# Eight PSUM banks dealt out anew in a hybrid attention kernel: three side banks and two maximum banks, with narrow pieces of several heads in one bank

## The reference, cut to what matters

```python
x = x + attn_a(_layernorm(x))   # scores = -|pos_q - pos_k| / 4, causal softmax, times V, projection
x = x + ffn(_layernorm(x))      # sigmoid(xr Wr^T) * (relu(xk Wk^T)^2 Wv^T), token shift
x = x + attn_b(_layernorm(x))   # 16 heads of 16: k, q, v = x Wkqv + b
                                # scores = q k^T / 4, causal softmax over keys, times v
x = x + ffn(_layernorm(x))
```

## Time and profile before

| | before |
|---|---|
| median of 3 executions | 2311.16 us (2307.39 to 2319.46) |
| the profiled execution, its own time | 2316.06 us |
| its span, first to last instruction | 2314.3 us |
| TensorE busy, share of the span | 83% |
| VectorE busy | 61% |
| ScalarE busy | 54% |
| GpSimd busy | 44% |

### The profile page before, as it was taken

One profiled execution on the slowest core, in us unless ns is written; L12 is line 12 of the kernel. 1 busy time (PEld: TensorE's weight loads), 2 busy tenths in 40 slices (PEclk: granted clock), 3 DMA queues, 4 the chain that ended last, 5 costly groups with the idle time before them and its releaser, 6 DMA issues. The chain is left out here.

```text
span 2314.3 us, 32515 instructions
## 1 busy us (share of the span) xinstructions
PE 1929.1 (83%) x9842; PEld 936.3 (40%) x9842; DVE 1417.5 (61%) x4173; ACT 1254.3 (54%) x2673; POOL 1024.2 (44%) x1074
## 2 busy tenths in 40 slices
PE   4477888888988899788987889888887889988986
PEld 3344343334433354324543345333443335432423
DVE  2336677567676666666765666756656666677642
ACT  0623654675537555394545755366554855555563
POOL 4454354335642455334743266423654246422414
PEclk8677899989998899989999899998999899999998
DMA  3006011310132111211122011231113111141100
GB/s 96 0 20 117 1 28 42 69 28 15 43 85 34 28 29 53 67 29 28 33 67 64 13 29 37 76 63 28 28 37 83 28 28 28 43 87 29 29 19 19
DMA packets 64347, 97.27 MB, mean 42 GB/s; under 512 B 15655, under 2 KB 58029, under 8 KB 58030
## 3 DMA queue, kind: packets, MB, share of 16 engines
q1 hardware_dynamic: 64174, 95.20, 18.6%
HBM read 61.09 MB, written 33.55 MB: 41 GB/s over the span
## 5 line engine op out<-in xcount | busy, mean ns | idle before, releaser
L852 ACT ACTIVATE pt<-exp_bank 128x512 f32<-128x512 f32 (+3 forms) x1536 | 742.5, 494 | 806.5 <-PE exp_bank L822 797.0
L867 DVE CUSTOM_DVE_ANT_0 max_bank<-max_bank,mask 128x128 f32<-128x128 f32 (+3 forms) x1024 | 500.3, 502 | 495.2 <-PE max_bank L811 478.2
L822 PE MATMUL exp_bank<-qs,ks 98*128 98x512 bf16 (+3 forms) x1536 | 523.8, 347 | 72.5 <-ACT pt L852 66.3
L811 PE MATMUL max_bank<-ks,qs 96*128 96x512 bf16 (+3 forms) x1536 | 525.0, 349 | 24.3 <-DVE piece_max L870 17.2
L870 DVE TENSOR_REDUCE piece_max<-max_bank 128x1 f32<-128x512 f32 x512 | 342.9, 686 | 164.7 <-PE max_bank L811 161.5
L837 PE MATMUL o_bank<-pt,v 128*17 128x512 f32 (+3 forms) x3072 | 346.2, 525 | 8.0 <-ACT pt L852 3.0
L889 POOL TENSOR_SCALAR_AFFINE_SELECT pt<-pt 128x512 f32<-128x512 f32 x256 | 170.1, 664 | 404.2 <-ACT pt L852 403.8
L353 POOL TENSOR_SCALAR xh<-xs,mv,rstd 128x256 f32<-128x256 f32 x256 | 322.6, 1266 | 10.0 <-PE side L379 3.8
L822 PEld LDWEIGHTS exp_bank<-qs,ks 98*128 98x128 bf16 x1536 | 153.9, 101 | 353.4 <-ACT pt L852 229.5
L811 PEld LDWEIGHTS max_bank<-ks,qs 96*128 96x128 bf16 x1536 | 154.7, 101 | 257.9 <-issue 102.1
L544 PE MATMUL side<-vp,p 128*128 128x260 f32 x576 | 185.2, 450 | 33.7 <-ACT p L473 18.3
(11 more groups left out here) (94 smaller groups left out, 2243.0 us busy)
## 6 DMA issues: line engine op xcount, KB each, us to landing
parts_dram<-parts SPq DMA_DIRECT2D x64, 384.0 KB, 2.6
qs<-parts_dram SPq DMA_DIRECT2D x192, 128.0 KB, 7.0
ks<-parts_dram SPq DMA_DIRECT2D x32, 384.0 KB, 4.8
xs<-in_L_attn_a_x_dram SPq DMA_DIRECT2D x16, 512.0 KB, 4.3
ks<-parts_dram SPq DMA_DIRECT2D x32, 256.0 KB, 5.5
out_dram<-xs SPq DMA_DIRECT2D x16, 512.0 KB, 3.1
ks<-parts_dram SPq DMA_DIRECT2D x32, 128.0 KB, 5.9
qs<-neg_maxT SPq DMA_DIRECT2D x64, 8.0 KB, 1.9
```

Of the source, the lines that this page charges most:

```text
L811: pe.matmul(max_bank[u % MAX_BANKS][:, 0:k1 - k0], qs[r][0:KROWS, j, P * tile:P * (tile + 1)], ks[r][0:KROWS, j, k0:k1], start=True, stop= ...
L822: pe.matmul(exp_bank[k % EXP_BANKS][:, 0:q1 - q0], ks[r][:, j, P * kt:P * (kt + 1)], qs[r][:, j, q0:q1], start=True, stop=True).then_inc(s ...
L852: act.activation(pt[:, e % 2, j, 0:q1 - q0], exp_bank[k % EXP_BANKS][:, 0:q1 - q0], ACT.Exp, scale=SCALE).then_inc(exp_done, 1)
L867: dve.tensor_tensor_reduce(scores, scores, mask[:, HALF - w:HALF], 1.0, LOWEST, ALU.add, ALU.max, piece_max[:, j, m:m + 1]).then_inc(max_f ...
```

## The change

The eight PSUM banks were 2 side, 3 maximum, 2 exponential and 1 output bank; they are 3 side, 2 maximum, 2 exponential and 1 output bank. The planner deals side jobs to three banks. In a group the 128-wide maximum pieces of all four heads are written to one bank, and the 256-wide ones of two heads to one bank. Into such a bank TensorE first writes a mask (the identity times a bfloat16 mask of 512 columns), then adds the heads' scores to it, all in the slot of the first of these heads; VectorE takes the maxima of all of them with one reduction over 512 columns. The wider pieces stay as they were, on two banks. A group has 38 jobs for the maxima in place of 48, of which 6 begin with the mask.

```diff
-MAX_BANKS, EXP_BANKS = 3, 2
+MAX_BANKS, EXP_BANKS = 2, 2
+MAX_HEADS = {}
+for m, (i, k0, k1) in enumerate(QUERY_PIECES):
+    together = HALF // (k1 - k0) if (k1 - k0) in (P, 2 * P) else 1
+    for j in range(0, GH, together):
+        MAX_HEADS[m, j] = range(j, j + together)
+MAX_JOB = {at: k for k, at in enumerate(sorted(MAX_HEADS))}
+MAX_JOBS = len(MAX_JOB)
...
-    free, before, shift, u = [BEGIN, BEGIN], BEGIN, 0, BEGIN
+    free, before, shift, u = [BEGIN, BEGIN, BEGIN], BEGIN, 0, BEGIN
...
-        side = [psum(f"side{k}") for k in range(2)]
+        side = [psum(f"side{k}") for k in range(3)]
+        maskb = sb("maskb", [P, 2, 2, P], BF16)
...
-                if u >= MAX_BANKS:
-                    pe.wait_ge(max_free, u + 1 - MAX_BANKS)
-                pe.matmul(max_bank[u % MAX_BANKS][:, 0:k1 - k0], qs[r][0:KROWS, j, P * tile:P * (tile + 1)],
-                          ks[r][0:KROWS, j, k0:k1], start=True, stop=True).then_inc(max_full, 1)
+                if (m, j) in MAX_JOB:
+                    heads = MAX_HEADS[m, j]
+                    k = MAX_JOBS * g + MAX_JOB[m, j]
+                    bank = max_bank[k % MAX_BANKS]
+                    if k >= MAX_BANKS:
+                        pe.wait_ge(max_free, k + 1 - MAX_BANKS)
+                    if len(heads) > 1:
+                        rows = maskb[:, :, :, :] if k1 - k0 == 2 * P else \
+                            maskb[:, 0, 1, :].unsqueeze(1).to_broadcast([P, GH, P])
+                        pe.matmul(bank[:, :], identb[:, :], rows, start=True, stop=False, skip_group_check=True)
+                    for h in heads:
+                        at = (h - j) * (k1 - k0)
+                        mm = pe.matmul(bank[:, at:at + k1 - k0], qs[r][0:KROWS, h, P * tile:P * (tile + 1)],
+                                       ks[r][0:KROWS, h, k0:k1], start=len(heads) == 1, stop=True,
+                                       skip_group_check=len(heads) > 1)
+                    mm.then_inc(max_full, 1)
...
-                scores = max_bank[u % MAX_BANKS][:, 0:w]
-                dve.wait_ge(max_full, u + 1).then_inc(scores_seen, 1)
+                if (m, j) in MAX_JOB:
+                    heads = MAX_HEADS[m, j]
+                    k = MAX_JOBS * g + MAX_JOB[m, j]
+                    scores = max_bank[k % MAX_BANKS]
+                    dve.wait_ge(max_full, k + 1).then_inc(scores_seen, 1)
+                    if len(heads) > 1:
+                        dve.tensor_reduce(piece_max[:, j:j + len(heads), m],
+                                          scores[:, :].rearrange("p (h n) -> p h n", h=len(heads)), AX.X,
+                                          ALU.max).then_inc(max_free, 1)
+                    elif k1 == P * (tile + 1):
...
+            pool.memset(maskb[:, :, :, :], 0.0).then_inc(cleared, 1)
+            pool.wait_ge(cleared, 4)
+            pool.affine_select(out=maskb[:, :, 1, :], in_=maskb[:, :, 1, :], compare_op=ALU.is_ge, fill=LOWEST, base=0,
+                               pattern=[[0, 2], [-1, P]], channel_multiplier=1).then_inc(consts_ready, 1)
```

More of the change, by code:

```diff
@@ L781, in sp_stack @@
                 copy(qs[r], 1, slot, part, 1)
-        emptied = [None, None]
+        emptied = [None, None, None]
         def side_of(*job):
@@ L863, in dve_att3 @@
                     dve.wait_ge(negmax_ready, g)
-                scores = max_bank[u % MAX_BANKS][:, 0:w]
-                dve.wait_ge(max_full, u + 1).then_inc(scores_seen, 1)
[L866 to L870, removed]
+                if (m, j) in MAX_JOB:
[8 more added lines that the diff above has]
+                    elif k1 == P * (tile + 1):
+                        dve.tensor_tensor_reduce(scores[:, 0:w], scores[:, 0:w], mask[:, HALF - w:HALF], 1.0, LOWEST,
+                                                 ALU.add, ALU.max, piece_max[:, j, m:m + 1]).then_inc(max_free, 1)
+                    else:
+                        dve.tensor_reduce(piece_max[:, j, m:m + 1], scores[:, 0:w], AX.X,
+                                          ALU.max).then_inc(max_free, 1)
                 if m == NP - 1 and j == GH - 1:
-                    dve.wait_ge(max_free, u + 1)
+                    dve.wait_ge(max_free, MAX_JOBS * (g + 1))
                     dve.tensor_tensor(piece_max[:, :, TPH:NT], piece_max[:, :, TPH:NT],
@@ L1034, in _ @@
                 pool.memset(v[:, :, :, HD:VW], 1.0).then_inc(consts_ready, 1)
-            pool.wait_ge(consts_ready, 8)
+            pool.wait_ge(consts_ready, 9)
             for r in range(STACKS):
@@ L1107, in _ @@
             dve.wait_ge(weights_ready, 1)
-            dve.wait_ge(consts_ready, 8)
+            dve.wait_ge(consts_ready, 9)
             def stage(at, s, n, h):
@@ L1160, in _ @@
             pe.wait_ge(weights_ready, 1)
-            pe.wait_ge(consts_ready, 8)
+            pe.wait_ge(consts_ready, 9)
             pe.wait_ge(rows_of_ones, STACKS)
```

## The result

The changed kernel takes 2180.53 us (median of 4; 2180.38 to 2181.95) against 2311.69 us before: a ratio of 0.943, 95% interval 0.9405 to 0.9456. The direction was right, the size was not.

A forecast was written before the change was run, and what follows sets the result against it. TensorE's own work plus its waits was taken as the bound. Side banks -100, masks +36, VectorE -10 and maximum banks +45 gave -29 us: 2,287 us for the profiled execution, 2,282 us median; range 2,225 to 2,345 us.

The forecast's parts named there:

- family of 14 entries: TensorE's side jobs waiting for the instruction that empties an earlier job's bank: 148.7 us listed, worth about 178 us.
- I take 70% of 178, 125 us, as removed: Side jobs: the third side bank removes 125 us of the 178 us of bank waits.
- I let a fifth come back: -100 us: Side jobs: a fifth of the 125 us removed returns as waits for ScalarE and VectorE, leaving -100 us.
- Rival 4: A lower clock in the attention slots; chance 0.05.
- The mask matmuls, "+36 us": 192 added mask matmuls on TensorE, 42 us at full clock, partly hidden in waits for ScalarE: +36 us.
- VectorE has 128 us less to do: Maximum reductions on VectorE: 260 us of reductions and accumulator reads go, 132 us of 512-column reductions come.
- the -10 taken: Lighter VectorE shortens the queue ahead of emptyings and reductions near m = 0, 1, 8 and 9: -10 us.
- Two maximum banks, +45 us: Maximum matmuls may run two ahead instead of three, so they wait for VectorE's reductions: +45 us.
- forecast 50 to 80: Sign to check: L811's maximum matmul waits for VectorE rise from 23 to 50 to 80 us.
- The count of bursts: 257 maximum matmuls start before the reduction two back ends, in about 100 bursts; worst slips sum to 53 us.
- rival 1: All 178 us of bank waits vanish, a tenth comes back: -109 us, 2,202 us; chance 0.10.
- Rivals 2 and 3: 2: removed waits return at ScalarE, within 0.5%, chance 0.17; 3: maximum banks become the wait, 2,357 us, chance 0.18.

The follow-up runs named there:

- side2_max2: Before with one maximum bank less (two in place of three) and nothing else: 2331.28 us, 1.0076 to before.
- side3_max2_old_plan: Before with three side and two maximum banks, unpacked, order and due slots of the plan for two side banks: 2149.09 us, 0.9295 to before.
- side3_max2: Before with a third side bank and one maximum bank less, planned for three side banks, no packing or masks: 2152.63 us, 0.9309 to before.
- side3_max2_no_mask: Three side and two maximum banks, unpacked, diagonal reductions by plain maxima without the causal mask: 2149.23 us, 0.9293 to before.

## Why the prediction was wrong, step by step

**What bounds the kernel: right.** TensorE and its waits; the family of 14 entries, read from the list and the timeline, was what the third bank removed.

**The sum again, by runs that change one thing at a time.** Median times, each step from the run before it:

| step | forecast | measured |
|---|---|---|
| one maximum bank less (before to side2_max2) | +45 | +18 |
| third side bank, order kept (side2_max2 to side3_max2_old_plan) | -100 | -182 |
| new plan (side3_max2_old_plan to side3_max2) | 0 | +4, within noise |
| packing with masks (side3_max2 to after) | +36 - 10 | +28 |

That is -132 us against a forecast of -29. Of the miss of about 103 us, 82 lie in the third side bank and 27 in the lost maximum bank. The steps depend on their order: the packing alone, on two side banks, was -5 us.

**"I take 70% of 178, 125 us, as removed" and "I let a fifth come back: -100 us": the term that failed.** It measured -182 us. The share removed was too small: side waits fell by 176 us with the order kept and by 179 from before to after, next to the 178 us worked out as the family's whole; 0 of 688 jobs, or 18 in the new plan, still meet the emptying of their bank. The share that comes back was too large: 14 of 176 us, under a tenth, in place of a fifth. (With the new plan it was 37 of 155 us, from side2_max2 to side3_max2, and the clock gave 66.) Where a wait was added and not removed (side2_max2), 51 of 63 us were absorbed, so "nothing comes back" is no rule either. The rows had a sign of it: in the stretch of the earlier trace rows VectorE is busy 11.85 and ScalarE 7.91 of 20 us. The prediction discounted this for stretches like the one with ScalarE at 19.80 of 20 us, without counting how many of the 14 entries lie in such a one.

**The clock: missing from the sum.** No term of the sum stands for a gain by it; of the chances only rival 4, a lower clock, has to do with it. The table books -55 us for it from before to after. The doubled matmuls brought the half clock in slots 24 to 47 from 89 to 24 us, and showed that this can save time: they were free there, and cost 28 us in slots 120 to 143. But it isn't a second gain of 55 us to be added to the forecast. Removing the side waits with the order kept gave only 18 us of it, and the 48 us that came with the new plan were paid back in waits (2149.09 and 2152.63 us). The packing alone took 55 us off the surcharge, three side banks with the new plan 59, and both together 55. This goes with what packing costs: -5 us on two side banks (surcharge -55), +19 us on three with the old plan (surcharge 130 to about 97), +28 us on three with the new plan (surcharge +4).

**The mask matmuls, "+36 us": right.** Leaving them out gave 33 us; 0.22 to 0.23 us each.

**"VectorE has 128 us less to do": wrong, though it decided little.** Its busy time fell by 39 us (1417.5 to 1378.9). The reads of the accumulator were counted in full, but each lies at the start of the next instruction: in the trace of before

```profile
1045.75 0.14 DVE L867 DVE_READ_ACCUMULATOR2_ANT piece_max<- 128x1 f32 x1
1045.77 0.31 DVE L867 CUSTOM_DVE_ANT_0 max_bank<-max_bank,mask 128x128 f32<-128x128 f32 x1
```

Without the 72 us of reads the groups that went and came give 74 + 108 - 133 = 49 us, and some other instructions on VectorE got longer. That leaving out the reads changes no time that can be measured is shown by side3_max2_no_mask. The relief at the maximum banks was larger than the -10 taken: 138 us before maxima unpacked, 110 packed.

**"Two maximum banks, +45 us": near in the waits, by two errors that partly cancel.** Before maxima the table has +58 us from before to after, where +45 less 10 were taken; the list of waits says 65 us, inside the forecast 50 to 80. But the lost bank by itself added 63 us there on two side banks, and 86 together with the third side bank and its plan, more than 45, and the packing took 28 off, more than 10. The count of bursts (53 us) was nearer the 63 than the 45 that was made of it. In time the lost bank alone cost 18 us, since 51 of the 63 came out of other waits.

**How near the better sum was, and by what luck.** With the family taken whole and nothing else changed the sum would have been -178 + 36 - 10 + 45 = -107 us, close to rival 1. With the +18 measured for the bank it would have been -134, next to the measured -131. That is in part luck: the 14 us that came back and the 18 us that the clock gave nearly cancel.

**The rivals.** Rival 1 was the nearest, 21 us too slow, and its mechanism is the one that the runs bear out: the whole family goes and about a tenth comes back. Rivals 2 and 3 fell: the wait for ScalarE stayed under 80 us and that at the maximum banks under 110. Rival 4, a lower clock in the attention slots, ran the other way: it rose from 0.94 to 0.96. One maximum bank fewer lowers it little: with one less and nothing else, the time at half clock went from 374 to 395 us of 2,331.

**Argued and not shown:** why the packing on two side banks raises the clock (248 us at half clock in place of 374). It puts 192 matmuls of 512 columns more on TensorE, which fits with the doubled matmuls, but no run here has the packing without the masks on two side banks. The stretch is another one, too: the packing took the half clock out of slots 0 to 23 (58 us to none) and left 82 of the 89 us in slots 24 to 47. Nor is it shown why the kernel with the new plan stands less at half clock than with the old one (241 and 357 us). And a third side bank beside three maximum banks was not run: with two exponential banks and one output bank it would take nine, where every kernel here has eight at most.

## What to carry to other kernels

A side job that begins in the slot in which its buffer is emptied makes TensorE wait until the other engine has come through that slot; one more buffer, so that reuse comes a slot behind, took nearly all of that wait away here (149 to 5 us on the list). If the waiting engine is the one that bounds and the others idle at the wait, start from the whole wait, and count in how many of the waits the others are busy before taking anything off. What the clock gives back is not simply added: here a plan with 48 us less of half-clock surcharge had as much more in waits. Give a bank from the buffers whose waits are absorbed elsewhere, and try the bank's move alone before the work that is meant to pay for it: here the move alone was 28 us faster than the whole change.

## What the runs showed of the hardware that was not expected

- Matmuls added in a stretch at half clock can be free: 192 of them, 32 us at full clock, cost nothing in slots of which 89 of 216 us were at half clock, and 28 us where 276 of 293 us were at full clock.
- In these kernels the time at half clock follows the order of the work more than the waits that the list shows: with 176 us of side waits removed and the order kept it fell from 395 to 357 us, with the new plan to 241 us, and the packing or the doubled matmuls alone brought 374 us down to 248 and 265 with the side waits still there.
- A higher clock need not be a shorter time: 357 and 241 us at half clock, 2149.09 and 2152.63 us.
- VectorE's reduction over 512 PSUM columns costs 686, 691 and 693 ns for one, two and four maxima.
- The accumulator's read after a masked maximum, 141 ns by its record, starts 0.02 us ahead of the next instruction and costs nothing that these kernels' times show: 2149.23 us without the 1,024 reads and their masks, 2152.63 us with them.
